# A perceiver block on one core: the two middle tiles written out in place of a loop

## The reference

```
x = x + xattn(layernorm(x), ctx, ctx)   # 16 heads of 16, softmax over 1601 keys, Wo, bo
x = x + attn(layernorm(x))              # 16 heads, causal over 64 tokens, out_proj
x = x + ffn(layernorm(x))               # router softmax over 8, top 2, gelu MLP 256-1024-256, all 8 computed
```

## Time and profile before

| what | value |
|---|---|
| median of 3 runs | 737.78 us (737.48 to 739.73) |
| the profiled execution's own time | 738.75 us |
| its span, first to last instruction | 736.7 us, 2.05 us less than its time |
| mean granted TensorE clock | 0.958 of full |
| tile 0, first scores to first scores of tile 1 | 54.42 to 152.00 us |
| tile 1 | 152.00 to 274.55 us |
| tile 2 | 274.55 to 404.56 us |
| tile 3 | from 404.56 us |
| last long stretch of PE, the experts | from 559.68 us, 172.26 us long |

### The profile page before, as it was taken

One profiled execution on the slowest core, in us unless ns is written; L12 is line 12 of the kernel. 1 busy time (PEld: TensorE's weight loads), 2 busy tenths in 40 slices (PEclk: granted clock), 3 DMA queues, 4 the chain that ended last, 5 costly groups with the idle time before them and its releaser, 6 DMA issues.

```text
span 736.7 us, 16650 instructions
## 1 busy us (share of the span) xinstructions
PE 668.6 (91%) x6576; PEld 549.2 (75%) x6584; DVE 498.7 (68%) x868; ACT 325.4 (44%) x517; POOL 226.2 (31%) x111
## 2 busy tenths in 40 slices
PE   2969999999999968999997999976897999999997
PEld 2648878878778846876885886654766898999996
DVE  4785687886748774774877757477556766676663
ACT  2434555554444533445453443445235443434431
POOL 2004566665535643643654644200000000000000
PEclk9988999999999988999998998999797999999999
DMA  6120120110110010001000000031400233112000
GB/s 227 58 68 2 25 67 24 27 44 24 25 44 24 24 26 23 23 24 46 24 24 23 2 1 2 1 116 40 189 1 1 115 115 116 69 45 114 0 0 28
DMA packets 12501, 34.16 MB, mean 46 GB/s; under 512 B 1483, under 2 KB 9812, under 8 KB 10260
## 3 DMA queue, kind: packets, MB, share of 16 engines
q1 hardware_dynamic: 12180, 31.62, 12.9%
q0 software_dynamic: 256, 1.58, 0.6%
HBM read 32.67 MB, written 0.52 MB: 45 GB/s over the span
## 4 chain that ended last, share of the span: by engine, by line
PE 79%; DVE 14%; issue 3%; ACT 2%; DMA 1%; SPq 0%; DVEq 0%; POOL 0%; ACTq 0%
PE bank L1015 44%; PE bank L1179 13%; PE bank L1024 8%; PE bank L1075 4%; DVE maxes L762 4%; PE bank L1118 2%; DVE ctx_lo L703 2%; PE bank L1109 2%; DMA bias_sb<-in_biases 1%; PE bank L1093 1%; ACT probs L638 1%; DVE shift L721 1%; DVE prob_sum L431 1%; DVE ties L810 1%; DVE masked L711 1%
## 5 line engine op out<-in xcount | busy, mean ns | idle before, releaser
L431 POOL TENSOR_TENSOR prob_sum<-probs,prob_sum 128x1024 f32<-128x1024 f32 x84 | 203.4, 2421 | 150.1 <-ACT probs L638 149.3
L638 ACT ACTIVATE probs<-bank 128x1024 f32<-128x1024 f32 (+1 forms) x104 | 106.6, 1025 | 140.4 <-PE bank L1179 137.2
L762 DVE TENSOR_REDUCE maxes<-bank 128x1 f32<-128x400 f32 (+1 forms) x256 | 131.5, 564 | 22.2 <-PE bank L1075 20.3
L620 ACT ACTIVATE h_raw<-bank,b_sb 128x512 f32<-128x512 f32 (+1 forms) x72 | 46.2, 642 | 106.8 <-PE bank L1015 106.7
L744 DVE SCALAR_TENSOR_TENSOR k_lo<-bank,bias_sb,k_hi 128x400 fp32r<-128x400 f32 (+2 forms) x64 | 40.5, 632 | 58.5 <-ACT k_hi L541 58.4
L1179 PE MATMUL bank<-qbd_hi,k_hi 64*128 64x256 f32 (+1 forms) x416 | 72.6, 343 | 7.5 <-issue 4.1
L1015 PE MATMUL bank<-w_hi,h_hi 128*128 128x256 f32 x256 | 72.9, 285 | 0.2 <-DVE h_lo L962 0.2
L1015 PE MATMUL bank<-w_hi,h_lo 128*128 128x256 f32 x256 | 72.6, 284 | 0.0
L1015 PE MATMUL bank<-w_lo,h_hi 128*128 128x256 f32 x256 | 72.5, 283 | 0.0
L961 DVE CAST h_hi<-h_raw 128x512 fp32r<-128x512 f32 (+1 forms) x72 | 28.5, 396 | 63.5 <-ACT h_raw L620 63.1
L1024 PE MATMUL bank<-probs,v_sb 128*32 128x128 f32 (+1 forms) x1664 | 69.1, 285 | 2.5 <-DVE masked L711 2.0
(11 more groups left out here) (157 smaller groups left out, 1452.2 us busy)
## 6 DMA issues: line engine op xcount, KB each, us to landing
raw<-in_w SPq DMA_DIRECT2D x16, 1024.0 KB, 6.8
ctx_raw<-in_ctx_t SPq DMA_DIRECT2D x16, 400.0 KB, 3.6
ctx_raw<-in_ctx_t SPq DMA_DIRECT2D x8, 402.0 KB, 3.6
ctx_raw<-in_ctx_t SPq DMA_DIRECT2D x8, 399.0 KB, 3.6
w_sb<-in_w_t POOLq DMA_DIRECT2D x1, 1280.0 KB, 9.5
x_all<-in_x SPq DMA_DIRECT2D x1, 512.0 KB, 3.8
w_raw<-in_w_t SPq DMA_DIRECT2D x1, 512.0 KB, 4.9
result<-x_all SPq DMA_DIRECT2D x1, 512.0 KB, 2.7
```

The source lines that it names most:

```text
L431: engine.tensor_tensor(prob_sum[0:ROWS[k], :], probs[0:ROWS[k], s % 2, :], acc[0:ROWS[k]], ALU.add).then_inc(summed, 1)
L620: nc.scalar.activation(h_raw[:, c % 2, 0:width], bank[:, at, 0:width], ACT.Gelu, bias=b1_sb[:, bass.ds(e, 1), c:c + 1].rearrange("p a b -> ...
L638: nc.scalar.activation(probs[0:ROWS[k], s % 2, :].rearrange("p (g n) -> p g n", g=G), bank[0:ROWS[k], 0:ROW_TILES, :], ACT.Exp, scale=SCAL ...
L762: nc.vector.tensor_reduce(maxes[:, g * PAIRS + j, c:c + 1], src[:, 0:width], AX.X, ALU.max).then_inc(read_dve, 1)
```

## The change

On PE, ACT, DVE and POOL the hardware loop over tiles 1 and 2 becomes a loop of the program that writes the kernel, so that both tiles stand in the instruction stream one behind the other, between tile 0 and tile 3. `t` becomes a plain number and the semaphore counts become constants, so the register instructions for them go. SP's loop over the tiles and the loops over the experts stay. No matmul, activation, vector operation, transfer or table of steps changes. The constant `TILE_LINKS` and the bookkeeping of `links` go, since the count now simply runs on.

```diff
@@ POOL
             tile(0, 2, {})
-            with pool.Fori(1, TT - 1) as t:
+            for t in range(1, TT - 1):
                 tile(t, 2, CHAIN_AT)
@@ ACT
             tile(0, FIRST, 2)
-            with act.Fori(1, TT - 1) as t:
+            for t in range(1, TT - 1):
                 tile(t, MIDDLE(t), 2)
@@ DVE
             tile(0, FIRST, 2, False)
-            start = links[0]
-            with dve.Fori(1, TT - 1) as t:
-                links[0] = start
-                links[1] = (t - 1) * TILE_LINKS
+            for t in range(1, TT - 1):
                 tile(t, MIDDLE(t), 2, True)
-            assert links[0] == start + TILE_LINKS, links[0] - start
-            links[:] = [start + (TT - 2) * TILE_LINKS, 0]
             tile(TT - 1, LAST, 1, True)
@@ PE
             tile(0, FIRST)
-            with pe.Fori(1, TT - 1) as t:
+            for t in range(1, TT - 1):
                 tile(t, MIDDLE(t))
             tile(TT - 1, LAST)
```

More of the change, by code:

```diff
@@ L41 @@
 RING = 5
-TILE_LINKS = 23
 K_UNITS = G * NC
```

## The result

The changed kernel takes 727.9 us (median of 5, 727.5 to 729.65) against 739.37 (median of 5) for the kernel before: a ratio of 0.9854, 95% interval 0.9839 to 0.9869. Two later timings gave 0.9864 (0.9844 to 0.9883) and 0.9849 (0.9836 to 0.9863). Forecast were 729.8 us and 8.0 us of gain. The time lies in the range; the gain is some 10.8 us by the ratio, 2.8 more than forecast.

What follows compares the result with a forecast made beforehand. PE was taken to bound the kernel, busy 91% of the span and carrying 79% of the longest chain. Turn 7.7 plus registers 0.3 gave 8.0 us, so 737.78 − 8.0 = 729.8 us, range 726.0 to 733.5.

Steps and rivals of the forecast that it cites:

- The turn: Where tile 1 meets tile 2 on PE: 5.10 us of stops plus 2.65 us of half clock, taken as 7.7 us gain.
- The registers: Register instructions removed from four engines in both tiles: 0.3 us gain taken, between nothing and 0.96 us.
- The four places of 0.10 us: Step 1 to step 2 in each of four sequences: 0.10 us saved at each, three counted.
- ACT's 0.14 us: At step 0, ACT's exponent starts 0.14 us later in the loop than in tile 3; claimed to be covered.
- The code stored twice: ACT, DVE and POOL fetch tile 2's code again; price nothing, since it is fetched ahead.
- The slower rival: Second middle tile: ACT, DVE and POOL stop for code, 3.29 us per fetch; up to 8.5 us slower, 746 us; chance 0.03.
- One sign that I had named: Instruction queue q14's packets grow by about five, while those on q8 hardly change.
- tile 3 and the experts come earlier by the sum and otherwise as they are: After tile 2: everything comes earlier by the 8.0 us sum, with nothing else changed.
- the main case's range: Whole kernel: 726.3 to 733 us around 729.8, from seam 0.3, registers −0.7 or +0.3, clock 2.65; chance 0.80.
- The low clock comes all the same: Behind the seam of tiles 1 and 2: half clock stays, only the stop goes; 5.4 us gain, 732.4 us; chance 0.09.
- The stop isn't the turn's: At the seam: PE waits for DVE's spreading of queries, so only 0.3 to 0.4 us gained, 737.4 us; chance 0.04.
- More than forecast: Router's chain: DVE's L806 and L810 part from POOL sums, 3.9 us per tile; 722 to 726 us; chance 0.04.

Runs made afterwards that it cites:

- the placement alone: Kernel before, loop kept, with the head of PE's loop body moved to the start of a fetch block: 733.35 us, ratio 0.9917.
- announcement and placement together: Kernel before, loop kept, with PE's branch named ahead and its loop head at a fetch block's start: 731.53 us, ratio 0.9906.
- the stop without a fetch: Changed kernel plus a 16-turn loop of one instruction on PE between tiles 1 and 2: 738.53 us, ratio 0.9993 to the kernel before.
- others written out: Kernel before with the tile loops of ACT, DVE and POOL written out, PE's loop kept: 738.01 us, ratio 0.9995.
- the short loop: Changed kernel plus an 8-turn loop of one instruction on PE between tiles 1 and 2: 732.75 us, one run.
- the turn announced: Kernel before, loop kept, with an instruction at the head of PE's body naming the branch at its end: 733.87 us, ratio 0.9939.
- PE alone: Kernel before with only PE's two middle tiles written out; ACT, DVE and POOL keep their loops: 729.91 us, ratio 0.9881.
- experts too: Changed kernel with the expert loops of PE, ACT and DVE written out too: 728.11 us, ratio 0.9859 to the kernel before.
- the gates later: Changed kernel with the router one step later in tiles 1 and 2, gates behind step 25's values: 728.3 us, ratio 0.9854 to the kernel before.

## Why the prediction was right, and where it fell short

**The turn.** 7.7 us was the term. From the traces: the seam takes 15.65 and 15.07 us in the two of before, and 7.35, 8.03 and 7.31 in the three of the changed kernel; the means are 15.36 and 7.56, so 7.8. It was right in size and in its two parts. The 3.29 and 1.81 us were two fetches (the placement alone removes the second; announcement and placement together leave 0.40 us of both), and the 2.65 us of half clock came from the stop (the stop without a fetch brings 2.55).

**The registers.** 0.3 us forecast, 0.6 measured by the lead, which grows from 0.60 to 0.93 us in tile 1 and from 9.23 to 9.53 in tile 2. The four places of 0.10 us are there in full, I had taken three; and a second kind of place, of about 0.1 us, is at step 25, probably PE's, which I had not looked for. ACT's 0.14 us was covered, as said.

**The code stored twice.** Nothing forecast, nothing measured. The slower rival is out: tile 2's stretches are as long as tile 1's, with the same busy times. One sign that I had named failed, without a price: q14 was to have some five packets more and has one more. Before, four arrived in tile 1 and none in tile 2; now two arrive in each. Without its register instructions a tile has less code to fetch.

**The step that was mis-sized** is the last of them, "tile 3 and the experts come earlier by the sum and otherwise as they are". They are not, in most executions. The steps 10 to 25 of tile 3 move by how the half clock falls on them. That stretch took 55.65 and 57.89 us in the kernel before, 57.92 to 58.03 in three others (others written out, head placed, long stop), 57.96 in the loop announced and placed, 55.64 with the short loop and 54.36 with the turn announced; and 56.21, 52.71 and 56.20 in the changed kernel, 52.74 and 52.72 in its two near kin (PE alone, experts too). The clocks of the timings tell how often: in 11 of the 14 executions of the changed kernel the mean clock is 0.966 or 0.967 and the time at most 728.5 us, as in the trace with 52.71; in three it is 0.962 and the time 729.3 to 729.9, as in the two traces with 56.2. In the trace of the common case the lead grows, from the last step of tile 2 to the end, by 2.1 us against the first trace of before and by 2.9 against the second; in the other two traces it changes by no more than 0.65 us either way. With 7.8 and 0.6 that makes up the 10.8 us. I had allowed for one half-clock stretch more or less in the range, at 2.65 us, but at nothing in the sum. (The terms of the main case's range, 0.3, 0.7 and 2.65, give 726.15 as its lower end and not 726.3; nothing hangs on it.)

**The time came closer than the gain, by luck.** 729.8 us is 1.9 from the 727.9 measured. But it was counted from a median of three, 737.78 us, and beside the changed kernel that of before was 739.37: a base 1.6 us too low hid part of a gain put too low.

**What stays open** is why the changed kernel meets the better case so often. The long stop isn't needed for the bad case: the loop announced and placed has 0.40 us of stop and 57.96 us. Nor is it only how late tile 3 begins: it began at 395.37 there, at 395.22 in the changed kernel with 56.21, and at 396.65 with 52.71. These are one trace each, and the experiments don't separate the position of the work from chance.

**The rivals.** "The low clock comes all the same" fell with the clock of 1.00 behind the seam. "The stop isn't the turn's" fell with PE written out alone. "More than forecast", by DVE's two slow operations parting from the POOL sums, fell too: they take 1.95 and 2.37 us in both middle tiles as before, and what came beyond the forecast came elsewhere. A turn to code at hand took 0.35 us, with the counting and the wait, and the turn of this body stopped PE for 5.10. The rule of the Trainium skill behind the second rival ("Advanced Engine Details and Errata", Control Flow Timing) gives about 108 ns for a compare-and-branch. That is a third of the first number and a 47th of the second. The rule of the Trainium skill on fetching ("Runtime: NRT & Kernel Launch", Instruction fetch mechanics) is that a taken branch to code no longer held waits for its fetch. The traces agree, with 5.10 us of stop at the turn before and none in straight code.

## What to carry to other kernels

When the engine that sets the pace has a hardware loop with a long body, look at the turn: a stop marked "issue" with instruction packets beside it, here in two pieces, and a slower clock behind it. The expert loops, whose bodies are shorter (276 matmuls a pass), cost nothing. Write the body out, or name the branch ahead and put the head at a block's start if the code must stay small; do it on the pacing engine, since the others' turns were free here. And count what a stop of that engine costs by the whole time: here 5.4 us of standing still cost 10.4 us.

## What the runs showed of the hardware that was not expected

- A taken branch back by two instructions cost PE 0.35 us, with the instructions that count and wait (2.44 us for seven, 5.37 for fifteen).
- The two stops at the turn sum to 5.1 us in all three traces of an unchanged PE loop (5.10, 5.12, 5.14), but how they divide varies from 3.29 and 1.81 to 3.71 and 1.41 in one program.
- The same program's tile 3 takes 52.7 or 56.2 us from step 10 to step 25 by the granted clock (0.97 or 0.88 in that stretch), from one execution to the next.
- DVE's L810 and L812 each take 0.22 us alone, and until the end of the POOL sum when they start just behind its start (2.37 us in the kernel before, 2.29 with the gates later), while the reciprocal beside such a sum keeps its 0.15 us.
